# Two recurrent layers with attention and FFN: the gate bias as a column operand of ScalarE's functions, and a changed opening of layer 1

## The reference

```python
# x [16, 128, 128] (batch, time, feature), cond [16, 128]
def lstm(x, h0, Wx, Wh, b):            # c starts at zero
    xp = einsum('ntd,df->ntf', x, Wx) + b
    for t in range(128):
        a = xp[:, t] + h @ Wh          # 4 gates of 128 columns: i, f, o, g
        c = sigmoid(f) * c + sigmoid(i) * tanh(g)
        h = sigmoid(o) * tanh(c)       # hs[t] = h
def attn(x, Wt, Wp, Wg):               # linear, no softmax
    return ((x @ Wt.T) @ (x @ Wp.T).T / sqrt(128)) @ (x @ Wg.T)
x = x + attn(lstm(x, cond, Wx1, Wh1, b1), W_theta, W_phi, W_g)
x = x + ffn(lstm(x, cond, Wx2, Wh2, b2), W1, b1, W2, b2)    # relu, 128 -> 512 -> 128
```

## Time and profile before

| | |
|---|---|
| median of 3 runs | 417.11 us (416.92 to 417.37) |
| the profiled execution | 414.27 us |
| its span, first to last instruction | 412.3 us |
| PE busy | 391.4 us, 95% |
| PE weight loads | 292.5 us, 71% |
| DVE busy | 273.1 us, 66% |
| ACT busy | 206.4 us, 50% |
| POOL busy | 8.1 us, 2% |
| mean granted clock of PE | 1.000 |

### The profile page before, as it was taken

One profiled execution on the slowest core, in us unless ns is written; L12 is line 12 of the kernel. 1 busy time (PEld: TensorE's weight loads), 2 busy tenths in 40 slices (PEclk: granted clock), 3 DMA queues, 4 the chain that ended last, 5 costly groups with the idle time before them and its releaser, 6 DMA issues.

```text
span 412.3 us, 14896 instructions
## 1 busy us (share of the span) xinstructions
PE 391.4 (95%) x4976; PEld 292.5 (71%) x4976; DVE 273.1 (66%) x1697; ACT 206.4 (50%) x1451; POOL 8.1 (2%) x20
## 2 busy tenths in 40 slices
PE   8999999999999999999999999999999999999996
PEld 5767666667666667666689877777777777777775
DVE  6776666666666666666668777666677666676664
ACT  4676554455554455554556444444444444444442
POOL 7000000000000000000000000000000000000000
PEclk9999999999999999999999999999999999999999
DMA  5111011111011111010000000000000000000000
GB/s 157 42 21 21 12 11 19 19 19 19 6 13 19 19 19 19 4 15 14 15 15 2 27 23 2 20 19 19 19 9 11 19 19 19 19 10 9 19 19 13
DMA packets 11696, 8.20 MB, mean 20 GB/s; under 512 B 1097, under 2 KB 11129, under 8 KB 11674
## 3 DMA queue, kind: packets, MB, share of 16 engines
q1 hardware_dynamic: 10842, 6.17, 7.6%
q0 software_dynamic: 544, 1.23, 1.0%
q10 hardware_dynamic: 288, 0.52, 0.4%
HBM read 2.87 MB, written 1.05 MB: 9 GB/s over the span
## 4 chain that ended last, share of the span: by engine, by line
PE 66%; DVE 17%; ACT 9%; issue 5%; DMA 2%; SPq 0%; DVEq 0%; POOLq 0%
PE fbank L413 21%; PE fbank L386 9%; DVE cell L1004 6%; DVE ring L1014 5%; ACT fgate L816 5%; DVE scan L1001 5%; ACT cell L834 5%; PE bankU L628 4%; PE bankV L407 4%; PE ibank L407 3%; PE gbank L407 3%; PE bankV L480 3%; PE bankY L635 2%; PE bankY L475 2%; PE bankU L513 2%
## 5 line engine op out<-in xcount | busy, mean ns | idle before, releaser
L413 PEld LDWEIGHTS fbank<-ring,whf 128*128 128x128 f32 x508 | 75.6, 188 | 77.8 <-DVE ring L1014 74.0
L386 PE MATMUL fbank<-warm_w 128*128 128x384 bf16 x534 | 123.8, 324 | 0.1
L816 ACT ACTIVATE fgate<-fbank 128x16 f32<-128x16 f32 x254 | 46.8, 184 | 139.4 <-PE fbank L413 139.0
L413 PE MATMUL fbank<-ring,whf 128*128 128x16 f32 x508 | 99.8, 272 | 15.1 <-DVE ring L1014 8.8
L1001 DVE TENSOR_TENSOR scan<-fgate,cell 128x16 f32<-128x16 f32 x254 | 43.8, 172 | 70.7 <-ACT fgate L816 63.1
L1014 DVE TENSOR_TENSOR ring<-cell,ogate_h 128x16 f32<-128x16 f32 x256 | 44.5, 174 | 41.7 <-ACT cell L834 41.4
L834 ACT ACTIVATE cell<-cell 128x16 f32<-128x16 f32 x256 | 43.0, 168 | 54.1 <-DVE cell L1004 53.8
L1004 DVE TENSOR_TENSOR_SCAN cell<-scan 128x32 f32<-128x32 f32 x256 | 59.4, 232 | 9.8 <-ACT scan L826 1.0
L407 PE MATMUL ibank<-h_hi,wh_parts 128*128 128x16 f16 x508 | 62.0, 169 | 0.0
L407 PEld LDWEIGHTS gbank<-h_hi,wh_parts 128*128 128x128 f16 x508 | 52.2, 137 | 0.0
L1019 DVE TENSOR_TENSOR h_lo<-ring,h_hi 128x16 f16<-128x16 f32 x256 | 44.8, 175 | 8.7
(11 more groups left out here) (189 smaller groups left out, 602.2 us busy)
## 6 DMA issues: line engine op xcount, KB each, us to landing
rows_t<-rows SPq DMA_DIRECT2D x16, 128.0 KB
x_rows<-in_x_dram SPq DMA_DIRECT2D x17, 64.0 KB
out_dram<-y_sb SPq DMA_DIRECT2D x16, 64.0 KB
xres<-x2T SPq DMA_DIRECT2D x15, 64.0 KB, 1.9
xin<-x2T SPq DMA_DIRECT2D x14, 64.0 KB, 1.8
w<-in_L_ffn_W_dram POOLq DMA_DIRECT2D x2, 256.0 KB, 4.2
wh<-in_L_cond_Wh_dram ACTq DMA_DIRECT2D x1, 256.0 KB, 2.8
wx<-in_L_cond_Wx_dram ACTq DMA_DIRECT2D x1, 256.0 KB, 3.7
```

The costliest lines, as they stand in the source:

```text
L386: nc.tensor.matmul(fbank[1 - p][:, P:4 * P], warm_w[:], warm_three, start=False, stop=True, skip_group_check=True)
L413: nc.tensor.matmul(step_out(p, t, GF), whf[layer][:], ring[:, (s - 1) % STEPS, :], start=False, stop=True, skip_group_check=True).then_inc ...
L816: nc.scalar.activation(fgate[:], fbank[p][:, NB * t:NB * t + NB], ACT.Sigmoid, scale=1.0 / Z_UNIT).then_inc(f_done[layer], 1)
```

## The change

The bias no longer goes through products and seeds. It is loaded as four rows, transposed on PE, kept as `bias_cols` [128, 4], and given to ScalarE's gate functions as a column. PSUM areas of g, i and o are cleared by copies of a zero tile; f's projection starts its area. The condition is the first DMA on SP. Steps 1 and 2 of layer 1 use float32 weights with unscaled h; the units and parts are made beside steps 0 to 2, those of i and o on GpSimd. The core of the diff:

```diff
-    FILL1 = [0, 4, 1, 2, 1, 4, 2, 4]
-    FILL2 = [2, 2, 1, 2, 2, 3, 2, 3]
+    FILL1 = [1, 4, 1, 2, 1, 4, 2, 4]
+    FILL2 = [2, 2, 2, 2, 2, 3, 2, 3]
...
+        def i_and_o(tile):
+            return tile.rearrange("p (a b n) -> p a b n", a=2, b=2)[:, :, 0, :]
...
         def _(sp):
+            sp.dma_start(cond_rows[:], cond).then_inc(cond_loaded, 16)
             sp.dma_start(x_rows[:, 0, :], x_ctb[0]).then_inc(rows_loaded[0], 16)
-            sp.wait_ge(bias1_cleared, 1)
-            sp.dma_start(bias[0][0:1, :], l1_b.unsqueeze(0)).then_inc(bias1_loaded, 16)
+            sp.dma_start(bias_rows[0][:], l1_b.rearrange("(g n) -> g n", g=4)).then_inc(bias1_loaded, 16)
...
         def _(pool):
-            pool.dma_start(cond_rows[:], cond).then_inc(cond_loaded, 16)
...
-            nc.gpsimd.memset(bias[1][:], 0.0).then_inc(bias2_cleared, 1)
...
+            pool.wait_ge(scale_made[0], 8)
+            nc.gpsimd.tensor_scalar(i_and_o(wh_parts[0][:, 0, :]), i_and_o(wh[0][:]), w_unit(0), None,
+                                    ALU.mult).then_inc(pool_parts, 1)
+            nc.gpsimd.tensor_scalar(i_and_o(wh_rest[:]), i_and_o(wh[0][:]), w_unit(0), None,
+                                    ALU.mult).then_inc(pool_parts, 1)
+            pool.wait_ge(pool_parts, 2)
+            nc.gpsimd.tensor_tensor(out=i_and_o(wh_parts[0][:, 1, :]), in0=i_and_o(wh_rest[:]),
+                                    in1=i_and_o(wh_parts[0][:, 0, :]), op=ALU.subtract).then_inc(pool_parts, 1)
+            pool.wait_ge(h_ready[0], 2)
+            nc.gpsimd.tensor_scalar(ring[:, 0:2, :], h_first[:], h_unit(0), 1.0 / Z_UNIT, ALU.mult,
+                                    ALU.mult).then_inc(first_kept, 1)
             pool.dma_start(w1[:], f_w1).then_inc(weights2_loaded, 16)
...
             def project_gate(layer, p, g, tile):
                 return nc.tensor.matmul(gate_out(p, g), wx[layer][:, gate_cols(g)], tile,
-                                        start=False, stop=False, skip_group_check=True)
+                                        start=g == GF, stop=False, skip_group_check=True)
...
+            def unscaled_step(s):
+                pe.wait_ge(h_ready[0], s)
+                for g, done in ((GF, f_ready), (GG, g_ready), (GI, i_ready), (GO, o_ready)):
+                    nc.tensor.matmul(step_out(0, s, g), wh[0][:, gate_cols(g)], h_first[:, s - 1, :], start=False,
+                                     stop=True, skip_group_check=True).then_inc(done[0], 1)
...
-            keep_warm(6)
+            keep_warm(4)
...
+            fill(0, 2)
+            pe.wait_ge(h0_kept, 1)
+            pe.wait_ge(wh1_loaded, 16)
+            initial(0, GG, start=True)
+            initial(0, GI, start=True)
+            fill(0, 1)
             pe.wait_ge(rows_loaded[0], 16)
             nc.tensor.transpose(bankU[:, 0:P], x_rows[:, 0, :], ident[:]).then_inc(x_transposed, 1)
-            top_product(0, fbank[1][:, 0:P])
             pe.wait_ge(bias1_loaded, 16)
-            bias_gate(0, 0, GG, start=True)
...
+            nc.tensor.transpose(cell[:, P:P + 4], bias_rows[0][:], ident[0:4, 0:4]).then_inc(bias1_transposed, 1)
+            top_product(0, bankY[:, 2 * P:3 * P])
             pe.wait_ge(xT_kept, 1)
             pe.wait_ge(wx1_loaded, 16)
...
             for s in range(STEPS):
-                if s == 1:
-                    pe.wait_ge(parts_ready[0], 3)
...
+                if s == 3:
+                    pe.wait_ge(parts_ready[0], 2)
+                    pe.wait_ge(pool_parts, 3)
+                if s in (1, 2):
+                    unscaled_step(s)
...
@@ scalar: the four gate functions of a step, fgate, g, i, ogate @@
                     nc.scalar.activation(fgate[:], fbank[p][:, NB * t:NB * t + NB],
-                                         ACT.Sigmoid, scale=1.0 / Z_UNIT).then_inc(f_done[layer], 1)
+                                         ACT.Sigmoid, bias=gate_bias(layer, GF), scale=1.0 / Z_UNIT).then_inc(f_done[layer], 1)
...
-            def seed(layer, p, kinds):
+            def clear(p, kinds):
                 for k in kinds:
-                    nc.scalar.copy(shared_cols(1 - p, SEEDED[k]), seeds[layer][:, k, :]).then_inc(seeded, 1)
+                    nc.scalar.copy(shared_cols(1 - p, SEEDED[k]), blank[:]).then_inc(seeded, 1)
...
@@ vector: beside steps 0 and 1 of layer 1 @@
+            def units_beside(s):
+                if s == 0:
+                    power_of(0, 3)
+                    inverse_of(0, 5)
+                    units_of(0, 6)
+                if s == 1:
+                    nc.vector.tensor_scalar(whf[0][:], wh[0][:, gate_cols(GF)], w_unit(0), None,
+                                            ALU.mult).then_inc(parts_ready[0], 1)
+                    dve.wait_ge(high_ready, 1)
+                    nc.vector.scalar_tensor_tensor(out=part(0, 1, GG), in0=wh[0][:, gate_cols(GG)], scalar=w_unit(0),
+                                                   in1=part(0, 0, GG), op0=ALU.mult, op1=ALU.subtract
+                                                   ).then_inc(parts_ready[0], 1)
...
+                if unscaled and s < 2:
+                    nc.vector.tensor_tensor(out=h_first[:, s, :], in0=tanhc, in1=ogate_h[:],
+                                            op=ALU.mult).then_inc(h_ready[layer], 1)
+                    return
```

More of the change, by code:

```diff
@@ L80, in build @@
         wh = [sb(f"wh{n}", [P, 4 * H]) for n in (1, 2)]
-        bias = [sb(f"bias{n}", [P, 4 * H]) for n in (1, 2)]
+        bias_rows = [sb(f"bias_rows{n}", [4, H]) for n in (1, 2)]
+        bias_cols = [sb(f"bias_cols{n}", [P, 4]) for n in (1, 2)]
         cond_rows = sb("cond_rows", [NB, H])
@@ L94, in build @@
         ogate_h = sb("ogate_h", [P, NB])
-        seeds = [sb(f"seeds{n}", [P, 3, P]) for n in (1, 2)]
+        blank = sb("blank", [P, P])
+        h_first = sb("h_first", [P, 2, NB])
         wh_parts = [sb(f"wh_parts{n}", [P, 2, 4 * H], f16) for n in (1, 2)]
@@ L246, in part @@
             return wh_parts[layer][:, which, gate_cols(g)]
[L248 to L255, removed]
+        def i_and_o(tile):
+            return tile.rearrange("p (a b n) -> p a b n", a=2, b=2)[:, :, 0, :]
+        PARTS = 3 + 2
         SCALED = 10
@@ L499, in beside1 @@
                     pe.sem_inc(scores_ready, 1)
+                if first and s == CH:
+                    pe.wait_ge(first_kept, 1)
                 if t == 0 and not (first and s == 0):
@@ L523, in beside1 @@
                 if first and s == 5:
[L524 to L529, removed]
+                    pe.wait_ge(bias2_loaded, 16)
+                    nc.tensor.transpose(bankU[:, 2 * P:2 * P + 4], bias_rows[1][:], ident[0:4, 0:4]
+                                        ).then_inc(bias2_transposed, 1)
+                if no_history:
+                    fill(0, (2, 1, 1, 2, 3, 4, 4, 3)[s])
                 else:
@@ L805, in set_layer2, with gate_bias, step @@
                 if s == 15:
+                    act.wait_ge(weights2_loaded, 64)
                     nc.scalar.mul(w1[:], w1[:], h_back(1)).then_inc(set2_ready, 1)
-            def step(layer, s, n, first=False, opening=False):
+            def gate_bias(layer, g):
+                return bias_cols[layer][:, g:g + 1]
+            def step(layer, s, n, opening=False):
                 p, t = s // CH, s % CH
@@ L875, in beside1 @@
                     nc.scalar.copy(queries[:], bankU[:, 0:2 * P]).then_inc(queries_kept, 1)
-                if first and 2 <= s <= 4:
-                    keep_seeds(s - 2)
             for s in range(STEPS):
-                step(0, s, s, first=s == 0, opening=s == 0)
+                step(0, s, s, opening=s == 0)
+                if s == 1:
+                    act.wait_ge(scale_made[0], 8)
+                    nc.scalar.mul(part(0, 0, GG), wh[0][:, gate_cols(GG)], w_unit(0)).then_inc(high_ready, 1)
+                    act.wait_ge(consts_ready, 3)
+                if s == 3:
+                    act.wait_ge(scale_made[0], SCALED)
                 beside1(0, s, first=True)
-                if s == 1:
-                    act.wait_ge(scale_made[0], SCALED)
-                if 2 <= s <= 4:
-                    keep_proj(s - 2)
+                if s in (3, 4, 6):
+                    keep_proj((3, 4, 6).index(s))
                 set_layer2(s)
@@ L1002, in step @@
                                             op=ALU.mult).then_inc(scan_inputs[layer], 1)
+                if unscaled and s == 1:
+                    fill_of(0, 8)
+                if unscaled and s == 2:
+                    pair_of(0)
                 dve.wait_ge(scan_inputs[layer], n * 3 + 3)
@@ L1052, in keep_first @@
             def keep_first(p):
+                dve.wait_ge(first_kept, 1)
                 nc.vector.tensor_copy(hist[:, p, :].rearrange("p (t b) -> p t b", b=NB),
@@ L1068, in _ @@
             for s in range(STEPS):
-                step(0, s, s, first=s == 0, opening=s == 0)
+                step(0, s, s, unscaled=s < 3, opening=s == 0)
```

(1 more changed line is left out.)

147 lines of the change are left out of this document (58 added, 89 removed).

## The result

The changed kernel takes 474.18 us (median of 6 runs, 473.83 to 477.46) against 417.01 us. The ratio is 1.1426, 95% interval 1.139 to 1.1463. The profiled execution took 473.89 us with a span of 471.2, against 414.27 and 412.3. The forecast was 480 us.

What follows compares the result with a forecast made beforehand. A chain of latencies, 1.550 us a step, was taken as the bound, not TensorE. Terms 64.3 + 0.1 - 0.1 - 1.2 = +63.1 us took the profiled 414.27 to 477.4; with 2.84 added, 480 us, range 471 to 491.

Steps and rivals of the forecast that it cites:

- The column's price and place: ScalarE's gate functions: a column lengthens each from 184 to 273 to 284 ns, i ends last; 252 steps cost +64.3 us.
- the spacing in the queue: ScalarE's queue f, g, i: overlap 0.10, so starts 0.18 apart; the scan starts at 0.675 us, not 0.42.
- my bound of 55.4: Low end in us of the 252 steps' term, from 0.22 us more per step; the upper end was 75.6.
- The opening: Start of layer 1: step 0 -1.62 us, steps 1 and 2 +0.37, parts sticking out +0.05; sum -1.2 us.
- Bias products and fill at no cost: TensorE's bias products replaced by fillers within both layers: 0, since the next step does not wait for TensorE.
- The passage between the layers: Between layer 1 and 2: removed bias product 0, longer i in layer 2's opening step +0.09 us.
- GpSimd: right that it fits: GpSimd's three 128x256 operations before step 3: 0.9 us floor, 2.7 us would just fit; cost taken as 0.
- Rival (a), the clock: TensorE's clock falls as steps lengthen: about 0.2 us a step, 50 us, so 530 us or 505; chance 0.12.
- My link between the longer step and the clock: TensorE: the step is 16% longer, busy share falls from 95% to about 82%, so the clock could fall.
- (b): ScalarE's queue: only one function's longer duration counts, 0.095 us a step, 24 us, giving 440 us; chance 0.06.
- (c): ScalarE's gate functions: the operand is free, fetched during waits; only the start counts, 415.9 us; chance 0.05.
- (d): The start gains nothing, GpSimd late or taking VectorE's memory access: 481 to 483 us; chance 0.77 together with the forecast.

Runs made afterwards that it cites:

- experiment 1: The changed kernel with the bias column taken from all four gate functions, both gate biases left out; ratio 1.0051 to the kernel before, median 415.88 us.
- experiment 2: The kernel before with a column of zeros as bias of its four gate functions; ratio 1.1383 to the kernel before.
- experiment 3: The changed kernel with the bias column kept on f's sigmoid alone, biases of g, i and o left out; ratio 1.0618 to the kernel before.
- experiment 8: Opening filler products: six in place of four in the changed kernel, ratio 1.1369; four in place of six in the kernel before, 1.0015.
- experiment 6: The changed kernel with a zero column as bias of tanh(c) as well; 491.97 us, ratio 1.1883 to the kernel before.
- e11_psum_bias_again: Changed kernel, no gate column, bias through PSUM, f's bias product in a chunk's step 1, fewer fillers, six opening products; 435.16 us, ratio 1.047 to the kernel before.
- experiments 5: The changed kernel with the bias column kept on g's tanh alone, biases of f, i and o left out; ratio 1.0478 to the kernel before.
- experiment 10: Changed kernel, no gate column, bias brought through PSUM by products and seeding copies, in two versions; 435.6 us (1.0464) and 435.16 us (1.047).
- experiments 7: The changed kernel with 10 more filler products in steps 0 to 7 of layer 1; ratio 1.1417 to the kernel before.

## Why the prediction was right

**The column's price and place: right.** f, g and i take 274, 269 and 277 ns, 90, 83 and 96 more than before, where the bounds were 89 and 100 more, 273 to 284. The scan waits for i. The sizes come from a scale and a Relu on 128x128, and they nearly held for functions of 128x16. Experiments 1 and 2 take the column out of one kernel and put it into the other: the 252 steps are 56 us shorter and 54 us longer. The figures of the Trainium skill ("ScalarE: Activation LUTs", section "What ACT_TABLE_LOAD costs") gave 65.5 us for the term, measured are 54.6: its 93 ns for the operand agree with f (90), its overlap of 93 ns is too small for this queue, where it is 0.10 behind f and 0.12 behind g and i.

**The mis-sized term: the spacing in the queue.** I took an overlap of 0.10, from a pair of conversions of 128x128 (0.09) and from g and i (0.11). It gives 0.18 between starts; the trace has 0.17 to 0.18 and 0.15. i ends 0.61 behind f's start, not 0.64, and the link is 0.64, not 0.675. The step grew by 0.217 us, not 0.255, and the term is 54.6 us, not 64.3. It lies under my bound of 55.4, but that bound was rounded: 0.60 + 0.035 - 0.42 is 0.215 and not 0.22, which makes 54.2 us, just under what was measured; the upper 0.30 is 0.287. Experiment 3 shows one fault in the reading: the starts of g and i in the earlier trace rows were arrivals of products, not the engine's spacing. A spacing says something of the engine only where nothing was awaited. Why it is 0.10 behind f and 0.12 behind g with the column is not shown.

**The opening: wrong by 5.6 us.** I forecast -1.2 us; it was +0.7 up to step 2 and +3.7 behind it. The DMAs did come first (the transposition at 3.32 in place of 5.17). The step that failed is that the products would run at 2.4 GHz as before. At 1.2 GHz the first projection comes at 6.27, and o's product is the late one. In experiment 1's execution the weight loads of the projections were 0.22 apart; the first projection came at 5.70, against my 5.2, and step 0 at 7.28, against my 6.90. So some 0.4 us of the miss was not the clock. Steps 1 and 2, forecast at 1.90 each, took 1.96.

**Bias products and fill at no cost: right.** Within a layer all steps behind 46 us are equal but step 21 (1.90) and those at the passage of a loop's body in layer 2 (1.83). The second kind comes with the column, not with the fill: experiment 2 has it too (1.81 to 1.84). Step 21 stands out in most versions of the changed kernel and in none of the kernel before, by 0.13 us here; what it waits for is open. The passage between the layers was +0.09 as forecast.

**GpSimd: right that it fits.** Its three operations took 2.6 us, near my upper figure of 2.7. They started 1.7 us later than I had put in, 9.73 to 12.33, and so did step 3, whose first product ran at 13.40.

**Rival (a), the clock, came true in part.** In this profile it is in the opening, not in the steady steps, which kept 2.4 GHz at 85% busy. Other profiles have short stretches later: six opening products (experiment 8) three times four steps of 1.96 to 2.25 us, with a granted clock of 0.66 from 80 to 90 us, and experiment 6 four steps of 1.97 to 2.29 at 268 to 272 and 285 to 289 us. Each stretch costs about 1 us or less, not the 50 us of the rival. My link between the longer step and the clock falls: experiment 1, with steps of 1.55 us, had a granted clock of 0.61 from 12 to 20 us too, and `e11_psum_bias_again`, with the same short steps, had such stretches up to 390 us. Rivals (b) and (c) fall by the spacing and by the wait of 0.32 to 0.69 us ahead of f that hid nothing. (d) came true in small: a scan of VectorE beside GpSimd took 0.08 us more here and 0.37 in experiment 1, below.

**The sum** was nearly right by luck, for two errors of opposite sign: -9.7 for the steps, +5.6 for the opening, together -4.1 of the 58.9 us of span. The other 2 us of the 6 between 480 and 474.18 come from the 2.84 us that I added from the profiled execution to the median; in the changed kernel these two lie 0.29 apart.

**Open:** what sets the level in the opening. It differs between executions of one kernel (the mean granted clock of the changed one is 0.978 to 1.000 over its six) and between versions with the same opening code, and four, six and more products made no difference that the runs can tell. That the rest of the change costs by this level is argued from the profiles, not shown.

## What to carry to other kernels

In a loop bound by latencies, an operand that looks free is paid on every function of the late branch: price one instruction from a row that has the operand (80 to 100 ns here), then add durations and spacings along the queue that is waited for. Put such work where an engine idles: as seeding copies off the chain the same column left the steps at 1.55 us but for one in eight (1.62). And an opening of 12 us can't be forecast to a microsecond while the matmul clock has two levels.

## What the runs showed of the hardware

A VectorE operation beside a GpSimd operation with two inputs is longer. Experiment 1, GpSimd and VectorE in the timeline:

```profile
10.24 0.67 POOL L351 TENSOR_TENSOR wh_parts<-wh_rest,wh_parts 128x256 f16<-128x256 f32 x1
...
10.40 0.60 DVE L1023 TENSOR_TENSOR_SCAN cell<-scan 128x32 f32<-128x32 f32 x1 [0.15 <-ACT scan L832]
```

The scan takes 0.23 in all other steps; here 0.37 us more, on the chain. It ends 0.09 us behind GpSimd's operation (11.00 and 10.91). So it does in the changed kernel (0.31 long, 12.42 and 12.33) and, 0.08 behind, in experiments 5 and 6; in experiment 3 VectorE's `whf` took 0.78 us beside it (12.52 and 12.44), where the kernel before, with no GpSimd arithmetic, has 0.28. That VectorE is held until GpSimd ends is a reading of these ends, not tested by a run of its own. On GpSimd a multiplication of 128x256 by a column took 0.93 us, longer than a subtraction of two tiles (0.67).

A pair of float32 products over 4 partitions held TensorE for 0.41 us, a pair over 128 partitions for 0.22 (experiment 10).

The granted clock of the records read 1.00 over stretches where the spacing of products was that of 1.2 GHz (experiments 7 and 8, and the changed kernel from 4 to 8.5 us). The spacing is the surer witness.
